# TensorE's build loop over chunk pairs, started half a pair earlier: the single first chunk moves into the loop, a branch skips the last half

## The reference

```python
agg = segment_sum(x[src], dst);  h = relu((x + agg) @ W1 + b1) @ W2 + b2          # layer 0
x = layernorm(x + x @ Wres + bres + h)
mean_agg(x) = segment_sum(x[src], dst) / max(deg, 1)                              # layer 1, twice
for _ in range(4):                                                                # layer 2
    h = x @ W_phi.T
    conv = x @ A.T + bias + dinv[dst] * segment_sum(w * dinv[src] * h[src], dst) + dinv**2 * h
    x = x + 0.1 * tanh(conv)
relu(segment_sum(x[src] @ W + b + edge_attr @ We + be, dst))                      # layer 3
```

## Time and profile before

| what | value |
|---|---|
| median of 3 runs (lowest to highest) | 1121.02 us (1120.48 to 1122.2) |
| the profiled execution | 1121.91 us, span 1120.1 us, granted PE clock 0.977 |
| PE busy | 1027.4 us (92%) |
| DVE, ACT busy | 520.1 us (46%), 284.9 us (25%) |
| the build on PE | from 77.0 us to 272 us of the span |
| chain that ended last | PE 85%, ACT 6%, issue 4%, DVE 2%, DMA 2% |

### The profile page before, as it was taken

One profiled execution on the slowest core, in us unless ns is written; L12 is line 12 of the kernel. 1 busy time (PEld: TensorE's weight loads), 2 busy tenths in 40 slices (PEclk: granted clock), 3 DMA queues, 4 the chain that ended last, 5 costly groups with the idle time before them and its releaser, 6 DMA issues.

```text
span 1120.1 us, 25031 instructions
## 1 busy us (share of the span) xinstructions
PE 1027.4 (92%) x10501; PEld 626.3 (56%) x10501; DVE 520.1 (46%) x945; ACT 284.9 (25%) x584; POOL 53.9 (5%) x73
## 2 busy tenths in 40 slices
PE   0246999998999999999999999999999999999997
PEld 0245877777755555455466455564455744457455
DVE  7487999994633356322323222332222334344333
ACT  0366999997500000010000000000000001112100
POOL 4500000001000000000000000000000000000000
PEclk9966999999999999999999999999999999999999
DMA  8214778788985856877569776598774987655931
GB/s 249 74 3 174 312 315 337 321 342 330 391 368 209 336 229 244 324 295 300 200 234 408 297 294 245 178 410 325 283 265 159 393 327 306 239 199 209 411 128 33
DMA packets 55910, 299.54 MB, mean 267 GB/s; under 512 B 7264, under 2 KB 10738, under 8 KB 52403
## 3 DMA queue, kind: packets, MB, share of 16 engines
q1 hardware_dynamic: 50352, 288.14, 66.5%
q0 software_dynamic: 3344, 9.67, 2.6%
q10 hardware_dynamic: 2160, 0.98, 0.4%
HBM read 235.93 MB, written 62.86 MB: 267 GB/s over the span
## 4 chain that ended last, share of the span: by engine, by line
PE 85%; ACT 6%; issue 4%; DVE 2%; DMA 2%; PEld 0%; ACTq 0%; SPq 0%; DVEq 0%; PEldq 0%
PE ps L1367 47%; PE ps L1360 18%; PE ps L1446 6%; PE ps L1470 5%; PE ps L1322 4%; PE ps L1277 2%; ACT arena L1102 2%; ACT arena L1103 2%; PE ps L1335 2%; DMA x_buf<-in_x 1%; PE ps L1209 1%; PE ps L1304 1%; ACT arena L1044 0%; PE ps L1266 0%; DMA arena<-in_dst_blocks,win_ati 0%
## 5 line engine op out<-in xcount | busy, mean ns | idle before, releaser
L1367 PE MATMUL ps<-arena 125*128 125x500 f32 (+2 forms) x700 | 267.5, 537 | 0.0
L1367 PE MATMUL ps<-arena,parts_even 125*128 125x500 f32 (+2 forms) x700 | 267.5, 537 | 0.0
L1367 PEld LDWEIGHTS ps<-arena,parts_even 125*128 125x128 f32 x700 | 129.4, 188 | 120.6 <-issue 106.7
L1367 PEld LDWEIGHTS ps<-arena 125*128 125x128 f32 x700 | 129.3, 188 | 120.5 <-issue 106.7
L1081 ACT ACTIVATE XT<-ps 128x500 f32<-128x500 f32 (+2 forms) x49 | 26.5, 540 | 491.9 <-PE ps L1335 491.9
L1360 PE MATMUL ps<-arena 125*128 125x500 f16 (+3 forms) x700 | 139.0, 352 | 1.6 <-DVE arena L761 1.3
L1102 ACT ACTIVATE arena<-ps 128x450 f16<-128x450 f32 (+1 forms) x187 | 119.4, 639 | 23.5 <-PE ps L1470 23.5
L1470 PE MATMUL ps<-arena 64*128 64x52 f16 (+1 forms) x6300 | 99.3, 179 | 24.4 <-issue 10.2
L1103 ACT ACTIVATE arena<-ps 128x450 f32<-128x450 f32 (+1 forms) x187 | 112.9, 604 | 0.0
L1470 PEld LDWEIGHTS ps<-arena 64*128 64x128 f16 x6300 | 89.4, 94 | 42.0 <-issue 21.2
L848 DVE TENSOR_TENSOR arena<-ps,dinv 125x512 f32<-125x512 f32 (+2 forms) x28 | 17.8, 634 | 202.6 <-PE ps L1322 202.6
(11 more groups left out here) (192 smaller groups left out, 738.9 us busy)
## 6 DMA issues: line engine op xcount, KB each, us to landing
arena<-weight_mats SPq DMA_DIRECT2D x20, 3250.0 KB, 11.1
arena<-weight_mats SPq DMA_DIRECT2D x20, 3000.0 KB, 10.6
arena<-count_mats SPq DMA_DIRECT2D x15, 3125.0 KB, 14.7
weight_mats<-arena SPq DMA_DIRECT2D x25, 1562.5 KB, 8.5
count_mats<-arena SPq DMA_DIRECT2D x25, 781.2 KB, 4.3
arena<-weight_mats SPq DMA_DIRECT2D x4, 2437.5 KB, 9.2
arena<-weight_mats SPq DMA_DIRECT2D x4, 2250.0 KB, 8.5
arena<-count_mats SPq DMA_DIRECT2D x3, 2343.8 KB, 9.5
```

What stands on the lines that cost most here:

```text
L1367: ins = t.matmul(o, xs[:, k, :], rhs, start=(k == 0), stop=(k == NC - 1))
```

## The change

PE's loop body is no longer a pair but the odd half of pair q followed by the even half of pair q+1. The loop runs from q = 0, so pair 0's odd half is in it and the straight code is gone. A branch on the counter (L1480) skips the even half in the last pass.

```diff
-                pe.sem_inc(agg0_done, 2)
+                pe.sem_inc(agg0_done, 1)
...
-                def pair(q, counts):
-                    for u in range(NO_UNITS if counts is None else 0, UNITS):
-                        if counts is not None:
-                            if u == LUMP_AT[0]:
-                                pe.wait_ge(counts_out, UNITS * q)
-                            if u in LUMP_AT:
-                                k0 = KCH * LUMP_AT.index(u)
-                                sum_counts(q - 1, counts, range(k0, k0 + KCH))
+                def chunk(q, odd):
+                    counts = (stg_all[0:NP, bass.ds((q + 1) % 2, 1), 0:STG_C // 2].bitcast(F16)
+                              .rearrange("p a (j k t) -> p (a j) k t", j=2, k=NC))
+                    for u in range(UNITS_OF[0], UNITS) if odd else range(0, UNITS_OF[0]):
+                        if u == LUMP_AT[0]:
+                            pe.wait_ge(counts_out, UNITS * q)
+                        if u in LUMP_AT:
+                            k0 = KCH * LUMP_AT.index(u)
+                            sum_counts(q - 1, counts, range(k0, k0 + KCH))
...
-                            if T == STEP_AT[step] or counts is None and T == TPC:
+                            if T == STEP_AT[step] or T == TPC:
...
-                pair(0, None)
                 pe.wait_ge(parts0_ok, 1)
                 pe.wait_ge(blank_ok, 1)
-                with pe.Fori(1, PAIRS) as q:
-                    pair(q, stg_all[0:NP, bass.ds((q + 1) % 2, 1), 0:STG_C // 2].bitcast(F16)
-                         .rearrange("p a (j k t) -> p (a j) k t", j=2, k=NC))
+                with pe.Fori(0, PAIRS) as q:
+                    chunk(q, 1)
+                    with pe.If(q < PAIRS - 1):
+                        chunk(q + 1, 0)
```

## The result

| | before | changed |
|---|---|---|
| median of 20 runs beside each other (lowest to highest) | 1122.22 us (1119.77 to 1123.79) | 1117.58 us (1111.1 to 1123.06) |
| profiled execution | 1121.91 us, span 1120.1 | 1111.1 us, span 1109.3 |
| granted PE clock in it | 0.977 | 0.981 |

A forecast was written before the change was run, and what follows sets the result against it. Bound: PE's chain of waits in the build, code loading in the first pass, then a PE-ACT ring of 14.16 us a pass. -5.2 + 3.3 = -1.9 us gave 1120.0 profiled, 1119.1 us median; range 1115.6 to 1124.0.

The forecast's parts named there:

- slow lumps: Lumps on PE at the low clock, one in four passes, 1.3 us each; the range allowed one more or less.
- First pass, -5.2 us: Code blocks fall elsewhere in the loop's first pass, so u2 of pair 2 comes at 109.2 instead of 114.39.
- the block behind 460: Code block behind matmul 460 of the new body: asked for at 88.2, there at 96.7, PE standing 5 us.
- The three lumps at 0: Lumps 3, 4 and 5 added to PE in pair 0, covered by waits for DVE: 0 us.
- The jump back, +0.30 us times 11: Jump back moves from u14/u0 to u7/u8, inside PE's part of the pace-setting chain: +3.3 us (0 to 6.2).
- The skip branch at 0: Branch at u14/u0, at most 0.28 us, covered by 0.65 + 0.21 us of waiting: 0.
- A: Rival: PE's queue of matmuls at the end of u7 covers the jump back; -5.2, 1115.8 us; chance 0.13.
- B: Rival: the packet for the block behind 339 comes behind pair 0's write; +1.8, 1122.8 us; chance 0.12.
- C: Rival: dear jump at u7/u8 (0.75 us a jump gives 1124.1), or two or three more slow lumps; chance 0.20.
- D: Rival: the jump back fetches its target's code, 4.0 us in each of 11 passes; 1160 us; chance 0.02.
- Lump 3 at 74.5: Sign of being right: PE starts lump 3 in pair 0 at 74.5 us, once `parts_even` is there.
- DVE's s0 of pair 3: DVE's step start after pair 2's three steps: claimed at 113.4 against 118.90, -5.5 us.

The follow-up runs named there:

- e1: The changed kernel run again with no edit, for its spread and a second profile: median 1117.05 us, ratio 0.9971 against before.
- e3: The changed kernel plus one extra write of the empty half to HBM, two units ahead of pair 0's write: median 1117.35 us, ratio 0.9974 against before.
- e4: The kernel before, straight code kept, with lumps 3, 4 and 5 added in pair 0: median 1117.57 us, ratio 0.9971 against before.
- e6: e4 with the write of pair 1's even half held back by four of ACT's units: median 1112.28 us, ratio 0.9903 against before.
- e11: The kernel before run once more, for a second profile: median 1121.59 us, ratio 1.0.
- e2: The changed kernel with pair 0's write issued four of ACT's units later: median 1113.5 us, ratio 0.9936 against before.
- e5: The changed kernel with the loop body u0 to u14 again, its even half skipped in the first pass: median 1114.04 us, ratio 0.9921 against before.
- e8: The changed kernel run a third time with no edit: median 1117.44 us, ratio 0.9953 against before.
- e12: The kernel of e5 run again: median 1112.97 us, ratio 0.9928 against before.
- e9: e5 with the waits of the build's entry moved into an else arm behind the skip: median 1117.28 us, ratio 0.9958 against before.

## Why the prediction was right, and where not

The sign and the range were right. The centre was 1.5 us too high as a time (1119.1 against 1117.58), and as a change half of what was measured (-1.9 against -3.8). That it is this near is in part luck: the first pass was missed by 5.7 us, and slow lumps (1.3), the rounds (0.8) and an open rest (1.7) took back two thirds of that. The terms came out so:

- **First pass, -5.2 us: wrong in size.** Measured is 31.84 against 42.7 (mean of the two profiles of before; the two differ by 1.55), -10.9. The step that failed is "the block behind 460 is asked for at 88.2, in the middle of this write, and comes ... at 96.7", and with it the stop of 5 us. I had put each request at the time at which PE's array does the matmul at the border. In the profile pair 0's write was issued at 84.05 and the packet of 85.0 went beside its start; PE met no late block at all. e1, whose build starts when before's does, shows it against the forecast's own times: the packet was moving at 88.0, when the forecast had it asked for, and not at 94 to 96, when the write was done. As I read it the sequencer reads ahead of the array by the queued work, up to a lump; the trace shows no request times, so that is argued from the packet times and not shown. That a packet behind a write does come late is shown (e3: a stop of 3.35 us), and e4 and e6 show that one beside its start can (above).
- **The three lumps at 0: wrong in sign.** They cost nothing, but they were worth 3.4 to 4.9 us of the first pass (e4): more work for PE where it would wait for code, and a clock that stays up. They needn't raise it: in the changed kernel's profile it rose at about 71 us, ahead of the first lump (72.57). Without lumps e11's had risen at 73 too and was back at half at 76.8. In e2 and e4, whose first lump ran at the low clock (2.26 us), it rose at about 79. In before's first profile it was at half until 95 (at 88 to 90 see the earlier trace rows). How much of the gain is clock and how much work isn't split by any run.
- **The jump back, +0.30 us times 11: right.** Passes are 14.46, and e5 gives 14.16 back with the jump under cover. Only the place on ACT differs: its idle time ahead of u10's copy has stayed at 0.20, and the loss stands ahead of u8's. ACT's rows in the changed kernel:

```profile
107.04 0.62 ACT L1102 ACTIVATE arena<-ps 128x450 f16<-128x450 f32 x1 [0.23 <-PE ps L1471]
...
109.22 0.61 ACT L1102 ACTIVATE arena<-ps 128x450 f16<-128x450 f32 x1 [0.20 <-PE ps L1471]
```

- **The skip branch at 0: right**, PE waits 0.64 us ahead of u2 as before.
- **Not in the centre: slow lumps and rounds.** Profiles of the changed kernel have 2, 4 and 4 slow lumps where before had 3 and 3; the rounds, with 847.6 against 845.92 and 847.65, add 0.8 on the mean.

The sum for e1 and e8, which start the build when before does: -10.9 + 3.3 + 1.3 (one slow lump more) + 0.8 = -5.5, and their spans are 5.35 below those of the two profiles of before (1114.95 against 1120.3). So the profiles are accounted for. The timed runs give 3.2 to 5.3 us (ratios of 0.9971, 0.9966 and 0.9953, intervals above), and what takes up to 2 us of it in runs without a profile is open; a late packet in some of them (R) would do it.

Of the rivals, A (jump covered) is refuted by the pass of 14.46. B (a packet loses its race) did not occur in the three profiles, though e3, e4 and e6 show that it can. C's dear jump (0.67 or more) is refuted; its slow lumps, two or three more, came as one more at most. D (code reloaded in each pass) is refuted by the window with q1 alone. "Lump 3 at 74.5" came at 72.57, which is 75.47 with the shift of 2.9 us; it waited for ACT's L1041 and not for `parts_even`, and cost nothing. DVE's s0 of pair 3 was forecast 5.5 us earlier. In the changed kernel:

```profile
68.02 3.48 DVE L703 SCALAR_TENSOR_TENSOR parts_even<-x_buf,parts_even 125x3200 f16<-125x3200 f32 x1
...
106.87 0.72 DVE L722 TENSOR_TENSOR arena<-arena 128x1092 f16<-128x1092 f16 x1
```

That is 38.85 behind L703 where before had 118.90 - 70.92 = 47.98, -9.1: less than PE's gain, since DVE, running without a pause here, is what is late next.

What stays open: what sets the number of slow lumps (1 to 4, at 1.33 us each, in kernels whose idle places differ little); whether the changed kernel's executions above 1121 us have a late packet (R); whether e3's stop reaches its median; and which of e5 and e6 is the faster for a reason. Both beat the kernel before, and their medians are under the changed one's (its ratios are 0.9953 to 0.9971): e6 with 1112.28 (0.9903, 0.9885 to 0.9921), e5 and e12 with 1114.04 and 1112.97 (0.9921, 0.9894 to 0.9948, and 0.9928, 0.9902 to 0.9953). Only e6's interval lies clear of all three of the changed kernel's. The two edits were not joined.

## What to carry to other kernels

A loop's first pass through long code has its own bound, the loading of the code: count its stops with "issue" before anything else, and see whether less straight code or useful or even empty work beside it takes them away. Put the jump back where the engine waits for another anyway; outside such a place it costs a fixed amount in every pass, here 0.30 us. Where code is loaded within some 0.3 us of a large write, one profile doesn't tell which of them comes first in the next execution. And compare stretches from a common row rather than whole spans: here 2.9 us of the profiled 10.8 lay ahead of everything the change touches.

## What the runs showed of the hardware

- A code packet can come late behind a write to HBM. Clear of writes the next packet came 4.0 us behind the one before (e2: 84.75 and 88.75); beside the start of a write after 3.75 (the changed kernel's first profile, e1), 5.0 (e4) or 8.25 us (e6). PE goes on 2.3 us after a late one: packet at 87.75, PE at 90.07 (e3); 101.5 and 103.77 (e4); 106.5 and 108.83 (before).
- A forward jump to code that isn't loaded stops PE for 5.44, 5.12 and 5.70 us (e5, e12, e9). Five blocks (some 80 KB) stay loaded: backward jumps over the whole body load nothing in 130 us. The Trainium skill (Runtime: NRT & Kernel Launch, Instruction fetch mechanics) expects a fetch on a taken branch out of the current two pages; the trace does not agree.
- A jump taken in the midst of PE's work costs 0.15 us (e9: passes of 14.31 against 14.16), a whole jump back with its register work 0.30 us (14.46); the same under a wait costs nothing (e5: 14.16).
- Executions of one kernel differ by 4 us (before, 20 runs) to 13.5 us (e8, 12 runs) here. The profiles find 5.9 us of it in the start of the build (L703 from 65.47 to 71.36) and up to 4.0 in the number of slow lumps.
